# Layer 0 of a two-layer gated attention kernel: another order of the pieces on four engines

## The reference, cut to what matters

```
x = x + tanh(g_xattn[0]) * L0_xattn(layernorm(x), ctx, masks, ...)   # 32 heads of 8, 8 key groups
x = x + tanh(g_ffn[0])   * L0_ffn(layernorm(x), w_up, w_down)        # Hadamard, 8-bit rounding, 256 -> 512 -> 256
x = x + tanh(g_xattn[1]) * L1_xattn(layernorm(x), ctx, ...)          # fp8 weights, 16 heads of 128
x = x + tanh(g_ffn[1])   * L1_ffn(layernorm(x), Wr, Win, Wout)       # router, 2 of 8 experts
```

```
q = X @ Wq.T + bq;  k = E @ Wk.T + bk;  v = E @ Wv.T + bv
scores = q k / sqrt(8), masked (causal and padding);  w = softmax(scores);  out = (w v) @ Wo.T + bo
```

## Time and profile before

| what | value |
|---|---|
| median of three runs | 1256.76 us (1254.0 to 1259.59) |
| the profiled execution, its own time | 1250.93 us |
| its span, first to last instruction | 1249.2 us |
| mean granted TensorE clock over the span | 0.963 |
| busy: PE, DVE, ACT, POOL | 1119.2, 1024.9, 944.2, 748.0 us |
| first piece F2 of a batch starts at | 72.99 us |
| batch 1 and batch 11 at their F2 | 89.05 and 246.98 us |
| last F7v of layer 0 starts at | 334.18 us |

### The profile page before, as it was taken

How to read it: one execution, slowest core, us unless ns; L and a number is a source line. 1 busy time by engine, 2 the same in 40 slices (tenths; PEclk the granted TensorE clock), 3 DMA queues, 4 the chain that set the end, 5 groups by cost and what they waited for, 6 DMA issues and landing times. The chain is left out here.

```text
span 1249.2 us, 30643 instructions
## 1 busy us (share of the span) xinstructions
PE 1119.2 (90%) x8831; PEld 906.0 (73%) x8831; DVE 1024.9 (82%) x2453; ACT 944.2 (76%) x3793; POOL 748.0 (60%) x1142
## 2 busy tenths in 40 slices
PE   3589899978899999999999999998999999669992
PEld 2356566545788888888888888887887888559981
DVE  6678888887898898898889899888789887766664
ACT  4777788869999989989998998997888778223330
...
GB/s 132 131 90 92 90 88 86 83 53 53 89 73 2 90 90 0 89 89 16 72 89 33 56 89 51 38 89 70 92 51 48 31 36 31 276 80 94 88 69 206
DMA packets 134168, 97.57 MB, mean 78 GB/s; under 512 B 54845, under 2 KB 127679, under 8 KB 134080
## 3 DMA queue, kind: packets, MB, share of 16 engines
...
## 5 line engine op out<-in xcount | busy, mean ns | idle before, releaser
L1557 POOL TENSOR_TENSOR head_rstd<-head_rstd,minus_half 128x4 f32<-128x4 f32 x192 | 225.7, 1175 | 15.0
L1545 ACT ACTIVATE squares<-ps 128x128 bf16<-128x128 f32 x768 | 202.5, 285 | 42.3 <-PE ps L1508 35.1
L1508 PE MATMUL ps<-w_proj_in,xq 128*128 128x512 f16 (+1 forms) x1024 | 209.6, 327 | 6.0 <-ACT headsT L1581 5.4
L1637 POOL TENSOR_TENSOR prob<-prob,rinv 128x512 f32<-128x512 f32 x128 | 140.5, 1098 | 107.6 <-DVE rinv L1632 107.4
L1581 ACT ACTIVATE headsT<-ps,l_hln 128x256 f32<-128x256 f32 (+1 forms) x256 | 168.2, 691 | 29.3 <-PE ps L1572 29.2
L1624 ACT ACTIVATE prob<-ps,nmax 128x128 f32<-128x128 f32 x512 | 182.7, 392 | 9.2 <-DVE nmax L1615 7.8
L1545 ACT ACTIVATION_READ_ACCUMULATOR squares<-ps 128x1 f32 x768 | 165.4, 216 | 0.0
L1565 DVE TENSOR_TENSOR heads_n<-ps,head_rstd 128x512 f32<-128x512 f32 x192 | 131.1, 683 | 25.0 <-POOL head_rstd L1557 24.8
L1508 PEld LDWEIGHTS ps<-w_proj_in,xq 128*128 (+1 forms) x1024 | 99.9, 98 | 53.1 <-issue 8.8
L1608 PE MATMUL ps<-headsT 128*128 128x128 f32 x1024 | 136.2, 276 | 1.0 <-DVE probT L1653 0.4
L1555 POOL TENSOR_TENSOR head_rstd<-head_squares,l_head_eps 128x4 f32<-128x4 f32 x192 | 45.8, 238 | 151.9 <-ACT squares L1545 151.2
...
## 6 DMA issues: line engine op xcount, KB each, us to landing
...
```

Source lines behind the costliest of these rows:

```text
L1508: last = e.matmul(out, xq[:, k, which, slot_at], weights(k, hl, c0, n), start=(k == 0 and hl == 0), stop=(k == KD - 1 and hl == 1))
L1545: last = e.activation(squares[:, 4 * n + h, :], A[n][:, h * HD1:(h + 1) * HD1], ACT.Square, scale=HD1**-0.5, accum_out=hss[:, 4 * n + h:4 ...
L1557: e.tensor_tensor(hr[:, four], hr[:, four], t["half"][:, four], ALU.pow).then_inc(g_r[n].sem, 1)
L1637: e.tensor_tensor(prob[:, kind, :, :], prob[:, kind, :, :], spread(rinv[:, kind, :], P), ALU.mult).then_inc(g_p[kind].sem, 1)
```

## The change

It gives the four computing engines another order in ORDER0, leaves SP's as it was, and cuts three POOL pieces in two so that other pieces can stand between their halves: F5v (the two steps of the Hadamard transform), WC (the subtraction, and then the product over 128x1024) and WL (two quarters each). No computation is added or left out. The strings in MIXED are rewritten for the new number of pieces. The lists of PE and POOL are now:

The core of the diff (F5v and WL are cut like WC; `...` marks what is left out):

```diff
-    "gpsimd": "XB+ F5v-- F1g- WL+ F3b- VC++ PD+ P1g++++ WC++ F7s-- F4v-",
+    "gpsimd": "F4v-- WC:1+ XB+ F5v:0-- F5v:1-- F1g- WL:0+ WL:1+ F3b- P1g++++ PD+ VC++ WC:0++ F7s--",
...
     @s.piece("WC", "gpsimd")
-    def _(e, i, p):
-        e.wait_ge(a_usum.sem, a_usum.at(i))
...
+    def _(e, i, p, n):
+        if n == 0:
+            e.wait_ge(a_usum.sem, a_usum.at(i))
...
+        else:
+            e.wait_ge(g_unit.sem, g_unit.at(i, 2))
+            byhead = unit[:, p, :].rearrange("p (h d) -> p h d", d=HD1)
+            e.tensor_tensor(byhead, byhead, spread(wscale[:, p, :], HD1), ALU.mult).then_inc(g_unit.sem, 1)
```

More of the change, by code:

```diff
@@ L279 @@
     "tensor": (
-        "PV:2- PV:3- NT ST:5- P2t++ F6--- ST:6- OB:0- F2t-- ST:7- P3++ S:0+ F3-- PV:4- PV:5- PV:6- PV:7- ST:0 "
-        "S:1+ ST:1 S:2+ F4-- ST:2 OB:1- F4u-- S:3+ ST:3 S:4+ OT- ST:4 S:5+ F7--- W- S:6+ S:7+ F7d--- PV:0 "
-        "PV:1"
+        "PV:2- PV:3- ST:6- NT F6--- F2t-- OB:0- ST:7- S:0+ F3-- PV:4- PV:5- PV:6- PV:7- ST:0 S:1+ S:2+ ST:1 F4-- "
+        "OB:1- ST:2 F4u-- ST:3 S:3+ OT- S:4+ P2t+++ PV:0 F7--- W- PV:1 S:5+ S:6+ ST:4 ST:5 P3+++ S:7+ F7d---"
+    ),
+    "vector": (
+        "MX:3+ MX:4+ P1++++ Wv- MX:5+ F1- MX:6+ MX:7+ F7v--- F2- NTl+ F6q-- NO:0 MX:0++ F3q- P3v+++ MX:1++ NO:1 "
+        "MX:2++ P2++++"
     ),
     "scalar": (
-        "EX:5 P2a+++ F2a- EX:6 EX:7 WM:0++ P3h+++ WM:1++ OC:1 EX:0+ EX:1+ F4a- EX:2+ F4s- OTa WH++ F7a-- EX:3+ NTh++ EX:4+ "
-        "OC:0+"
-    ),
[L288 to L291, removed]
-    "gpsimd": "XB+ F5v-- F1g- WL+ F3b- VC++ PD+ P1g++++ WC++ F7s-- F4v-",
+        "P2a+++ WH+ EX:4 P3h+++ OC:0 NTh+ F2a- EX:5 EX:6 WM:0++ EX:7 WM:1++ OC:1 EX:0+ EX:1+ F4a- EX:2+ F4s- OTa "
+        "EX:3+ F7a--"
+    ),
+    "gpsimd": "F4v-- WC:1+ XB+ F5v:0-- F5v:1-- F1g- WL:0+ WL:1+ F3b- P1g++++ PD+ VC++ WC:0++ F7s--",
     "sync": "INS- ROW-- INT- LW OUT CT++",
@@ L690, in layer0 @@
     d_unit, a_usum = sig("d_unit", "sync", 16 * len(UNIT_PARTS)), sig("a_usum", "scalar", 2)
-    g_unit, a_uhigh, g_ulow = sig("g_unit", "gpsimd", 3), sig("a_uhigh", "scalar"), sig("g_ulow", "gpsimd")
+    g_unit, a_uhigh, g_ulow = sig("g_unit", "gpsimd", 3), sig("a_uhigh", "scalar"), sig("g_ulow", "gpsimd", 2)
     def row(i):
@@ L1081, in _ @@
     @s.piece("F5v", "gpsimd")
-    def _(e, i, p):
[L1083 to L1089, removed]
+    def _(e, i, p, n):
+        if n == 0:
+            e.wait_ge(a_hid.sem, a_hid.at(i))
+            e.tensor_tensor(fly[:, 0:4:2, :], hid[:, 0:4:2, :], hid[:, 1:4:2, :], ALU.add)
+            e.tensor_tensor(fly[:, 1:4:2, :], hid[:, 0:4:2, :], hid[:, 1:4:2, :], ALU.subtract).then_inc(g_fly.sem, 1)
+        else:
+            e.wait_ge(g_fly.sem, g_fly.at(i, 1))
+            e.wait_ge(pe_h2.sem, pe_h2.at(i - 1))
+            e.tensor_tensor(hidT[:, 0:2, :], fly[:, 0:2, :], fly[:, 2:4, :], ALU.add)
+            e.tensor_tensor(hidT[:, 2:4, :], fly[:, 0:2, :], fly[:, 2:4, :], ALU.subtract).then_inc(g_fly.sem, 1)
     @s.piece("F6", "tensor")
@@ L1165, in _ @@
     @s.piece("WC", "gpsimd")
-    def _(e, i, p):
-        e.wait_ge(a_usum.sem, a_usum.at(i))
[L1168 to L1174, removed]
+    def _(e, i, p, n):
+        if n == 0:
+            e.wait_ge(a_usum.sem, a_usum.at(i))
+            e.tensor_tensor(wsum[:, p, :], wsum[:, p, :], share[:, :], ALU.mult).then_inc(g_unit.sem, 1)
+            e.wait_ge(g_unit.sem, g_unit.at(i, 1))
+            centred = unit[:, p, 0:CENTRED * HD1].rearrange("p (h d) -> p h d", h=CENTRED)
+            e.tensor_tensor(centred, centred, spread(wsum[:, p, :], HD1), ALU.subtract).then_inc(g_unit.sem, 1)
+        else:
+            e.wait_ge(g_unit.sem, g_unit.at(i, 2))
+            byhead = unit[:, p, :].rearrange("p (h d) -> p h d", d=HD1)
+            e.tensor_tensor(byhead, byhead, spread(wscale[:, p, :], HD1), ALU.mult).then_inc(g_unit.sem, 1)
     @s.piece("WH", "scalar")
@@ L1181, in _ @@
     @s.piece("WL", "gpsimd")
-    def _(e, i, p):
+    def _(e, i, p, n):
         e.wait_ge(a_uhigh.sem, a_uhigh.at(i))
         high, low = (t["wb"][:, hl, bass.ds(i, 1), :].rearrange("p u c -> p (u c)") for hl in (HI, LO))
-        for c0 in range(0, UNIT, UNIT // 4):
+        for c0 in range(n * UNIT // 2, (n + 1) * UNIT // 2, UNIT // 4):
             some = slice(c0, c0 + UNIT // 4)
@@ L1203, in starting @@
             ("scalar", "WH", 0, 0): ("rows1",), ("scalar", "EX", 0, 0, 0): ("rows2",),
-            ("gpsimd", "P1g", 1, 1): ("blocks",), ("gpsimd", "VC", 0, 0): ("more", "masks"), ("gpsimd", "WC", 0, 0): ("ready",),
+            ("gpsimd", "P1g", 1, 1): ("blocks",), ("gpsimd", "VC", 0, 0): ("more", "masks"), ("gpsimd", "WC", 0, 0, 0): ("ready",),
             ("gpsimd", "XB", 0, 0): ("gated",),
@@ L1209, in starting @@
             ("vector", "P1", 1, 1): ("ready", "unit0", "more"), ("vector", "P2", 1, 1): ("unit1",), ("vector", "P1", 2, 0): ("masks",),
-            ("vector", "NTl", 1, 1): ("late",), ("vector", "NO", 0, 0, 0): ("late2",),
+            ("vector", "MX", 1, 1, 5): ("late",), ("vector", "NO", 0, 0, 0): ("late2",),
             ("vector", "MX", 0, 0, 4): ("gated",), ("vector", "P1", 4, 0): ("rows",),
@@ L1216, in starting @@
         steps = [("begin",)] + [one for step in steps for one in [(name,) for name in ahead.pop((owner, *step), ())] + [step]]
-        assert not [key for key in ahead if key[0] == owner]
+        assert not [key for key in ahead if key[0] == owner], [key for key in ahead if key[0] == owner]
         return steps
@@ L2204 @@
     "tensor": (
-        "aaaaaaaaaaaaaaaaaaaaaaaaaaaaaaaabaaaaaaaaaabaaaaaaaaaaaaaaaaaaabaaaaaaaaaaabbaaaaabaaababaaabbababab"
-        "ababbbbabababbbbababbbbbbbbbbbbbbbbbbbbbbbbbbbbbbbbbbbb"
-    ),
[L2208 to L2211, removed]
+        "aaaaaaaaaaaaaaaaaaaaaaaaaaaaaaaaaaaaaaaaaaaaaaaaaaaaaaaaaaaaaaaaaaaaaaaaaaaaaaaaaaaaaaaaaaaaaaaaaaaa"
+        "aaaaabaaaaaaaaaabaaaaaaaaaaaaaaaaaaabaaaaaaaaaaabbaaaaabaaababaaabbabababababbbbabababbbbababbbbbbbb"
+        "bbbbbbbbbbbbbbbbbbbbbbbbbbbb"
+    ),
+    "vector": (
+        "aaaaaaaaaaaaaaaaaaabbaaaaaaaaaaaaabaaabaaaaaaaabaaaaabbbabbbaaaabaababbacbaaacaabbbabbbbbcbcbabbabbb"
+        "abbbbbbbbcbbbbbbbbcbbbbbbbbbbbbbbbbcbbbbbbbbbbbcbbbbbbb"
+    ),
+    "scalar": (
+        "aaaaaaaaaaaaaaaaaaaaaaaaaaaaaaaaaaaaaaaaabbbaaaabaaabaaabaabaabbaabcaaaabaabababaababccbbbacbbbbabab"
+        "abbbccbbbabbbbbbbbbbcbbbbbbbbcbbbbbb"
+    ),
+    "gpsimd": (
+        "aaaaaaaaaaaaaaaabaaaaaaaaaaaaabaaaaaaaaabbaabaabababaaababaabbbaabbabbbbbbbbbbbbbbbbbbbbbbbb"
+    ),
+    "sync": (
+        "aaaaaaaaaaaaabaccccbccbcc"
+    ),
 }
```

## The result

The changed kernel takes 1305.46 us (median of 4 runs, 1304.4 to 1308.94) against 1257.61 us before: a ratio of 1.0389, interval 1.0357 to 1.042. It is slower, as forecast, but by more than the range allowed (1284 us, 1265 to 1299). The profiled span is 1302.7 us against 1249.2 us, 53.5 us more.

A forecast was written before the change was run, and what follows sets the result against it. It took a loop of waits through POOL (VC, F3b, F3, four PV) to set the 15.79 us turn. Ten turns at 18.51 us add 27.2 us, start and end cancelling: 1256.8 + 27 = 1284 us, range 1265 to 1299.

The forecast's parts named there:

- The loop and its PE leg: New order's turn: F6 to DVE, P2, P2t, then PE without a gap to F6; PE leg 8.90 us.
- The lone PV: On PE, a PV followed by another kind of product holds PE 0.97 us; three places add 1.85 us a turn.
- The term of 4.92 us from MX:0 to P2: On DVE, the pieces from MX:0 until P2 is ready, read from the kernel before: 4.92 us.
- the prediction's own zero: The end of F6, from which the forecast counts all times of the turn on PE, DVE and POOL.
- P2 inside the product: P2 on DVE, ready at 8.15 us, waits out POOL's product over 128x1024 (7.56 to 9.46 us): 1.46 us.
- the forecast of 18.51: Steady turn of 18.51 us instead of 15.79: P2 ends at 9.61 us, then the PE leg of 8.90.
- the sum: The turn's terms: 0.20 to DVE, 3.03, 4.92, P2 at 1.46, and 8.90 on PE, giving 18.51 us.
- The start: First 89 us of layer 0: batch 1 put 0 to 4 us later, cancelled against the end.
- The end: End of layer 0, the turn at 247 us: 0 to 4 us given back for a lighter PE.
- What VC's wait became: On POOL, VC no longer waits 2 us at the end of a full turn; POOL idles over 4 us.

The follow-up runs named there:

- pv_together: Changed kernel with PV:0 and PV:1 put back beside PV:2 and PV:3 on PE; 1293.33 us, ratio 1.0291.
- b_torn: Kernel before with PV:0 alone behind OT and PV:1 alone behind W on PE; 1272.18 us, ratio 1.0129.
- wc_behind: Changed kernel with POOL's subtraction (WC:0) behind F4v and its product over 128x1024 (WC:1) behind XB; 1298.00 us, ratio 1.0335.
- scale_early: Changed kernel with the feed-forward weight scale earlier on DVE: reduction ahead of MX:3, rest ahead of MX:5 of batch 1; 1299.37 us, ratio 1.0345.
- b_relief: Kernel before with P1g and PD ahead of VC on POOL; 1258.73 us, ratio 1.0006.
- rest: Changed kernel with PV together, ST:6 behind F2t, NTh ahead of EX:4, wc_behind's and scale_early's edits, P3 left as changed; 1272.38 us, ratio 1.0138.
- p3_back: Changed kernel with P3 back between ST:7 and S:0 on PE and P3h behind WM:1 on ACT; 1293.57 us, ratio 1.0298.
- both: Changed kernel with the edits of pv_together and wc_behind at once; 1282.99 us, ratio 1.0202.
- all_back: Changed kernel with the edits of pv_together, wc_behind, scale_early and p3_back at once; 1272.44 us, ratio 1.0133.
- best: Changed kernel with all_back's edits, but ST:6 behind F2t, NTh ahead of EX:4, weight scale placed as before, P3 between S:0 and ST:7; 1291.95 us, ratio 1.0288.

## Why the prediction was wrong

- **The loop and its PE leg: right.** The turn is F6, F6q, P2, P2t, PE, F6. The PE leg was put at 8.90 us and is 9.20. The lone PV was put at 0.97 us and is 0.97 to 0.98; tearing alone costs 1.18 us a turn in the order of before. Shown by pv_together and b_torn.
- **The term of 4.92 us from MX:0 to P2: wrong, 6.23 us in five of the ten turns.** It was read from a turn in which q of F3q was free. I followed POOL against P2 alone. By the prediction's own zero VC starts at 4.58 us, so the subtraction at about 5.1, and q comes at about 5.4: the meeting could have been worked out. It costs 1.29 us (1.58 against 0.29 in wc_behind). In the other turns the term is right (4.94 us in four of the five).
- **P2 inside the product: right in five turns, displaced in the other five.** In the turn shown first the product was put at 7.56 to 9.46 us and lies at 7.47 to 9.37. P2 was put at 8.15 and came at 9.48, since q had been held; it took 0.72 us instead of 1.46. Where q is free P2 is caught as forecast (1.39 us), and four of those turns, 18.8 to 19.0 us, are within 0.5 us of the forecast of 18.51. The turn shown first, with q held, is 19.53: against the sum 1.31 us more from MX:0 to P2, 0.74 less for P2, 0.30 more on the PE leg, 0.02 more up to MX:0, and 0.13 for the step from P2 to P2t, which the sum put at nothing. The mean is 19.34 us, 8.2 us over the forecast in ten turns.
- **The start: the largest miss of a single step.** I wrote "0 to 4 us later" and cancelled it; it is 11.9 us to batch 1. I had looked at which piece the weight scale stands behind on DVE, and not at the small product that waits for it on PE with S:5 to S:7 behind. scale_early gives 5.15 us of it back; what makes the rest stays open, the lower clock there included.
- **The end: 6.2 us later in the trace where I gave back 0 to 4; not shown to be a loss.** Every other trace here, that of b_relief with the time of before among them, also takes 4.6 to 9.3 us more than the trace of before from batch 11 to the end of the span. That trace is of an execution 6.7 us under its median, and the medians leave 0.6 us for the end. So it may be that this one execution was quick there.
- **What VC's wait became: wrong in a detail.** I wrote that VC would no longer wait for 2 us; it waits 1.91 us, because PE is late too, though the wait no longer sets the turn. DVE does wait 0.80 us at MX:7 for S:7, but longer, 1.21 us, for W behind the lone PV:0.

So two steps failed: the DVE term, in which q was taken as free and meets POOL's subtraction, and the start, put at nothing on balance. The ten turns (8.2 us, of which 3 are the PE leg's 0.30) and the start (11.9 us) make 20.1 of the 21.5 us between 1284 and 1305.46. Of the 3.55 us by which a turn is longer, 2.87 came back with the PV together, EX:4's chain loosened and POOL's two large pieces moved (rest). The last 0.68 us are not taken apart. P3 on the PE leg can be most of them, since two pairs of runs (the changed kernel and p3_back, both and all_back) put its place at about 0.6 us. That is not shown: best, the one run with all of this undone, met another wait.
